# Register loads of the weight offsets spread over the slots of a loop's turn

## The reference, cut to what matters

```python
x = x + attention(layernorm(x))          # 4096 tokens, width 128, 16 heads, linear attention
x = x + ffn(layernorm(x))

def ffn(x):                              # per token
    logits = x @ router_w.T              # 16 experts
    top_vals, top_idx = top_k(logits, 2)
    gates = sigmoid(top_vals)
    for each of the 2 chosen experts e:
        gate, up = split(x @ gate_up_w[e])       # 128 -> 2 * 128
        moe += gates * ((silu(gate) * up) @ down_w[e])
    shared = (silu(x @ sg.T) * (x @ su.T)) @ sd.T    # a shared expert of width 256
    return moe + shared
```

## Time and profile before

| | |
|---|---|
| three runs | 313.11, 315.89, 319.80 us (median 315.89) |
| the profiled execution | 313.39 us, its span 311.5 us |
| mean granted TensorE clock | 0.893 of full speed |
| PE busy | 238.9 us (77%) |
| DVE busy | 163.4 us (52%) |
| ACT busy | 126.6 us (41%) |
| POOL busy | 122.9 us (39%) |
| the item loop | about 165 to 281 us |

### The profile page before, as it was taken

The page is one execution under the profiler, slowest core; times in us unless marked ns, Lnnn a source line. Parts: engine busy times, 40 slices in busy tenths (PEclk is TensorE's granted clock), DMA queues, the critical chain, the costliest instruction groups (busy, mean ns, idle before and its releaser), DMA issues.

```text
span 311.5 us, 5386 instructions
## 1 busy us (share of the span) xinstructions
PE 238.9 (77%) x1334; PEld 189.6 (61%) x1335; DVE 163.4 (52%) x759; ACT 126.6 (41%) x341; POOL 122.9 (39%) x132
## 2 busy tenths in 40 slices
PE   6999974779486859677988678777887967886960
PEld 2477753667365647335787666666776856764850
DVE  4778975364737462524444443453454444443496
ACT  2968771646361612140024444343444344341210
POOL 0000073717272727274400465446344444655000
PEclk9999997859687968796799999999799799996995
DMA  8999930101010101013923233232233232111794
GB/s 246 432 224 221 320 114 18 51 17 45 27 51 17 54 27 52 17 51 95 121 50 90 79 99 97 70 85 77 61 87 81 68 85 77 42 42 36 265 383 169
DMA packets 26842, 33.06 MB, mean 106 GB/s; under 512 B 4531, under 2 KB 21046, under 8 KB 26694
## 3 DMA queue, kind: packets, MB, share of 16 engines
q1 hardware_dynamic: 18934, 21.16, 23.9%
q0 software_dynamic: 4096, 8.46, 8.6%
q10 hardware_dynamic: 3792, 3.21, 4.1%
HBM read 15.74 MB, written 12.75 MB: 91 GB/s over the span
## 4 chain that ended last, share of the span: by engine, by line
PE 64%; issue 16%; DVE 9%; ACT 5%; another core or an unknown queue 4%; DMA 1%; DVEq 0%; ACTq 0%
PE pQ L1189 6%; PE pZ L1189 6%; PE pKVN L1045 6%; PE pN L1197 3%; PE pKVN L1197 3%; PE pN L1005 3%; PE pKVN L1005 3%; PE pKV L1015 3%; PE pT L1183 3%; PE pN L1096 3%; PE pN L1061 2%; PE pKV L1035 2%; PE pKVN L1204 2%; PE pZ L1079 2%
## 5 line engine op out<-in xcount | busy, mean ns | idle before, releaser
L383 POOL DMA_INDIRECT routed<-ZB,ROWS x64 | 61.5, 961 | 91.1 <-DVE ROWS L711 74.0
L400 POOL DMA_INDIRECT results<-Y x64 | 61.3, 957 | 73.4 <-DVE Y L843 54.0
L838 DVE SCALAR_TENSOR_TENSOR Y<-pN,XS,Y 128x128 f32 x40 | 14.0, 351 | 32.6 <-PE pN L1197 10.1
L838 DVE SCALAR_TENSOR_TENSOR Y<-pKVN,XS,Y 128x128 f32 x40 | 14.0, 351 | 31.2 <-PE pKVN L1197 10.4
L1189 PE MATMUL pQ<-WF,attT 128*128 x80 | 26.3, 411 | 4.9 <-ACT attT L498 3.3
L1189 PE MATMUL pZ<-WF,attT 128*128 x80 | 26.7, 416 | 3.1 <-issue 2.9
L498 ACT COPY attT<-pT 128x256 f32<-128x256 f32 (+1 forms) x42 | 15.2, 363 | 29.1 <-PE pT L1183 11.2
L498 ACT COPY attT<-pN 128x256 f32<-128x256 f32 (+1 forms) x41 | 15.1, 368 | 24.5 <-PE pN L1183 13.4
L1045 PE MATMUL pKVN<-WA,XNT 128*128 128x256 f32 x64 | 22.3, 509 | 0.0
L1105 PE MATMUL pZ<-chosen,tri 128*128 128x64 bf16 x8 | 1.6, 200 | 23.1 <-issue 22.7
L1045 PEld LDWEIGHTS pKVN<-WA,XNT 128*128 128x128 f32 x64 | 15.8, 258 | 3.4 <-ACT XNT L441 0.5
(11 more groups left out here) (192 smaller groups left out, 569.8 us busy)
## 6 DMA issues: line engine op xcount, KB each, us to landing
XS<-routed SPq DMA_DIRECT2D x80, 65.0 KB
Y<-pad SPq DMA_DIRECT2D x1, 4160.0 KB
WF<-w_ffn SPq DMA_DIRECT2D x1, 3456.0 KB, 14.5
ZB<-results SPq DMA_DIRECT2D x6, 512.0 KB, 6.0
X<-x SPq DMA_DIRECT2D x8, 256.0 KB, 5.7
routed<-pad SPq DMA_DIRECT2D x25, 65.0 KB, 13.2
out<-X ACTq DMA_DIRECT2D x6, 256.0 KB, 2.2
routed<-ZB,ROWS POOLq DMA_INDIRECT x64
```

Source lines behind the costliest of these rows:

```text
L383: nc.gpsimd.indirect_dma_start(routed, bass.IndirectOffsetOnAxis(ap=ROWS[:, q, t, k:k + 1], axis=0), Z[:, q, t, k, :], None).then_inc(scat ...
L400: nc.gpsimd.indirect_dma_start(results, bass.IndirectOffsetOnAxis(ap=Y[:, b * YROW + D:b * YROW + D + 1].bitcast(U32), axis=0), Y[:, b * Y ...
L838: nc.vector.scalar_tensor_tensor(part, pY[j % 2], XS[:, j, D + 1:D + 2], part, ALU.mult, ALU.add).then_inc(s_y, 1)
```

## The change

PE reads 5 offsets at the head of a turn instead of 20. Then in each of the slots 0 to 14, behind `down`, it reads one more, for the slot after the next needs of `gate_up` and `down` (`w[j + 5]`, which is in use from slot j + 2 on). DVE reads 4 block offsets at the head and 4 more at the head of slots 4, 8 and 12. Nothing else is changed: the same values come into the registers, and the engines' work and its order are the same.

```diff
@@ VectorE
             def body(it, first):
-                y = values(dve, table[0:1, T_Y, bass.ds(it * BODY, BODY)], BLOCKS * YROW)
+                y = []
                 for j in range(BODY):
                     n = it * BODY + j
+                    if j % 4 == 0:
+
+                        y += values(dve, table[0:1, T_Y, bass.ds(it * BODY + j if j else it * BODY, 4)], BLOCKS * YROW)
                     if not (first and j < YLEAD):
                         gather(n - YLEAD, (j - YLEAD) % BODY, y[j])
@@ TensorE
-            def experts(it, count):
-                return values(pe, table[0:1, T_EXP, bass.ds(it * BODY, count)], (EXPERTS - 1) * F_EXP)
+            def experts(it, first, count):
+                return values(pe, table[0:1, T_EXP, bass.ds(it * BODY + first if first else it * BODY, count)],
+                              (EXPERTS - 1) * F_EXP)
@@
             def body(it, first):
 
-                w = experts(it, BODY + WLEAD)
+                w = experts(it, 0, WLEAD + 1)
                 for j in range(BODY):
@@
                     if not (first and j < 4):
                         down(n - 4, (j - 4) % BODY, w[j])
+                    if j < BODY - 1:
+
+                        w += experts(it, j + WLEAD + 1, 1)
                     if not first and j == 1:
@@
-            w = experts(TURNS, WLEAD)
+            w = experts(TURNS, 0, WLEAD)
```

## The result

| | before | with the change |
|---|---|---|
| median of 20 runs each | 314.37 us | 314.44 us |
| lowest and highest | 311.12, 319.80 | 311.43, 318.10 |
| ratio, 95% interval | | 1.0066 (1.0036 to 1.0096) |

The two medians are the same within 0.1 us; 311.9 us was forecast. The ratio of 1.0066, 2.1 us, takes in undisturbed runs alone, while over all 20 runs of each kernel the means are 314.79 and 314.55 us, so whether the change makes the kernel slower at all hangs on which runs are left out. What is clear is that nothing like the forecast 4.0 us was won. The profiled execution of the changed kernel took 316.72 us, its span 314.9.

The account below looks back on a forecast made before the run. PE was taken to set the pace, its head waits (5.8 us) being time of the span. Heads -4.8 us and DVE's loads +0.75 made -4.0: 315.89 to 311.9 us, range 308.5 to 316.5.

Parts of the forecast that it names:

- The price of a load: PE's register loads: 73 ns per entry and 47 besides, so 411 ns for five entries and 120 for one.
- 75 single loads on PE: Fifteen a turn between `down` and the next slot's transposes: 0.12 us each, hidden behind queued matmuls, counted as 0.
- The room of 0.3 us: Time PE's sequencer has spare for a load in a slot with no gap, read at 179.2 us: 0.3 us.
- The heads of PE: Start of each turn: shorter loads give 1.09 us at four later heads, 0.4 at turn 0, -4.8 us together.
- DVE at the head: DVE's shorter load lets the turn's first `hidden` come just in time for PE, at worst 0.15 us late: counted as nothing.
- 15 loads of four on DVE: Loads inside the turns, 480 ns each, make `gather` 0.1 us late in about half the slots: +0.75 us.
- the rival that made them the cause: DVE's loads inside turns cost 621 ns, all fifteen without slack: +3.3 us, 314.4 us in all; chance 0.17.
- The sum: Whole kernel: -4.8 us from the heads and +0.75 from DVE's loads, -4.0 us, so 311.9 us.
- The rival of the stops: Stops in turns 2 and 3 are fixed in time, so two or three heads give nothing: about 314.5 us; chance 0.17.
- The rival of a fixed price: PE's single loads have a latency that doesn't shrink with entries: at 0.47 us each, +2.4 us, 318.2 us; chance 0.07.
- The rival of the clock: Shorter idle times keep one or both slow-clock turns at 2.4 GHz, one giving 1.7 us more: 309.4 us; chance 0.12.
- the alternative sum of -2.4: With the skill page's 200 ns per register, a head's load takes 1.0 us and each head gives only 0.5 us.

Follow-up runs that it names:

- held loop: Item loop with POOL's scatters held back until all items are done: 87.5 us in the kernel before, 87.3 us in the changed kernel.
- singles_twice_again: Changed kernel with a second single load behind each of PE's fifteen a turn, on the chip without stops: 250.94 us, 1.0383 to before.
- held pair: Kernel before and changed kernel, both with POOL's scatters held back until all items are done: programs 361.76 and 361.66 us, loops 87.5 and 87.3.
- pe_alone: Kernel before with only the PE part of the change, DVE's loads as before: 315.22 us, 1.011 to before.
- pe_fours: Kernel before with PE reading four entries at the head and behind `down` in slots 0, 4, 8, 12, DVE as before: 313.82 us, 0.999.
- singles_twice: Changed kernel with a second single load behind each of PE's fifteen a turn, on a chip with stops: 317.63 us, 0.9941 to before.

## Why the prediction was wrong

**The price of a load failed, and with it the sum.** The prediction drew a line through 4 entries (338 ns) and 20 (1502 ns) and read off 411 ns for five and 120 for one. The price goes by accesses of up to four: five entries are two accesses (591 to 600 ns), one entry is one (302 ns). The hint was in rows named as the other end: DVE's 5 entries at 621 ns lie at nearly twice PE's four, and its 16 at 1130 below four times 338. They were read as DVE's own line.

**75 single loads on PE**, taken as nothing, are the other step that failed. The room of 0.3 us was right: in the held loop the slots of 0.87 us in the hardware turns keep their length with loads of 0.30. But the room was read in a slot in which the sequencer has a lead, and taken for all. Behind a head it has none, and slot 1, with a piece behind the load, loses 0.44 to 0.55 us a turn. `singles_twice_again` shows the edge: one load more and 3.8% are lost.

**The heads of PE**, -4.8 us in the sum: the four later heads give 0.74 to 0.82 us each in the held pair, not 1.09, which is the price again (1.38 us of load became 0.59). Turn 0 gives 0.64, where 0.4 was counted. Together 3.8. That the heads' waits would go was right, 5.8 to 0.8 us.

**DVE at the head**, "just fits": in the held loop it does, with 0.4 us to spare at the head shown. At the head of the changed kernel shown at 208.5 it does not: there L1186 waited for `hidden` and came 0.45 us behind L1183, because DVE's load (at 207.7, 341 ns) stands in front of the turn's first `gather` and `hidden`. How often that happens in the loop with stops, and what it costs the program, was not tried apart.

**15 loads of four on DVE**, +0.75: they take 345 ns, in a room predicted as 0.4, and in the held loops slots 4, 8 and 12 keep their 0.87 us in the hardware turns. +0.75 was too much, and the rival that made them the cause is out.

**The sum**: -0.8 us in the held loop (0.2 between the first and the last transposes, 0.6 at the head of turn 0), for -4.0. The heads give 3.8 instead of 4.8, and 3.0 are given back in the slots behind them and in turn 0, where 0.75 was counted for DVE and nothing for PE.

**The program with the stops** is another matter. On the chip without stops the change makes no difference (1.0016, 0.9975 to 1.0057). Where the stops are, 112 to 116 us of loop hold 87 of work, and the time does not follow PE: 7 us more of loads cost 1.9, a PE without loads won nothing. The rival of the stops (chance 0.17) came nearest in its number, 314.5 us, but the held pair shows that hardly anything is won without stops either. The rival of a fixed price (chance 0.07) had the mechanism, a load that doesn't get cheaper with fewer entries, but took it at 0.47 us and in half of all slots, where it is 0.30 us and a few slots pay. Whether the change is slower at all on the chips with stops, and why doubled loads came out on the faster side there, stays open; after a stop all sequencers are without a lead, so single loads might be exposed more often (pe_alone at 1.011 beside pe_fours at 0.999 points that way, singles_twice at 0.994 against it). The rival of the clock looked for less of the lower level; the one trace of the changed kernel shows more of it.

That the measured median lies inside the stated range of 308.5 to 316.5 us is no merit of the mechanism: no change at all from the 315.89 us that the sum started from would lie in it too, and that base, a median of three runs, stood 1.5 us above that of twenty. Two smaller slips: the alternative sum of -2.4 is that of the heads alone and would be about -1.65 with the 0.75; and with that 0.75 the single load at which the gain is used up is 0.41 us, not 0.43.

The Trainium skill's 200 ns per register ("Runtime: NRT & Kernel Launch", section on instruction fetch mechanics) lies between the 120 ns predicted for one entry and the 302 measured, but taken per register it fits neither 302 ns for one nor 330 for four.

## What to carry to other kernels

Price a register load from rows with different counts before spreading it, and spread it in whole accesses (here four entries): what one long load costs at a head, many short ones can cost again. Room in a sequencer is to be read in the slot in which it has no lead (behind a branch, a long wait, a head), not in the steady one. When a head is shortened on one engine, look at what the next engine has in front of the work that is waited for. The kernel that keeps the gain has both a shorter load on PE with no load in slot 1, and `hidden` ahead of DVE's load; which of the two is worth how much was not tried apart. And where a loop is much longer than its engines' work, hold back the suspected engine once, and measure edits in both loops.

## What the runs showed that was not expected

- One TENSOR_LOAD of 1 entry took 302 ns in the middle (PE), of 4 entries 330 to 345 (PE and DVE), of 5 591 to 621 (PE and DVE), of 16 1096 to 1357 (DVE; 1099 on PE), of 20 1357 to 1568 (PE). The first loads of the loop are dearer: five entries 802 on PE, four 594 on DVE.
- With POOL's scatters of 0.96 us each in the loop, ACT and DVE stand still for about 3 us once or twice in most turns on three chips (with the clock that falls behind it, 25 us of 112), and not at all on a fourth (89.4 us of loop), where the same kernel takes 241.6 us instead of 314 to 319. The loop is only part of that: on the fourth chip the first stage ends at 120 us instead of 165, with a granted clock of 1.00 up to 119 us where the kernel before has 0.87 in its trace. By what means the scatters stop ACT and DVE no run shows, and what differs between the chips was not found.
